# The expert layer as one block with its two norms: top four by the 8-largest instruction, token shares spread over partitions by transfers, the store in pieces

## What is computed

```python
x = _layernorm(x + _L1_attn_ref(x, ...))
# _L1_ffn_ref, x is (2048, 128):
scores = sigmoid(xt @ gate_w.T)                    # 16 experts
_, idx = lax.top_k(scores + gate_b, 4)             # of equal values the lower index wins
w = take_along_axis(scores, idx); w = w / sum(w) * 2.5
comb = zeros((T, 16)).at[arange(T)[:, None], idx].add(w)
for e in range(16):                                # w13 (128, 128), w2 (128, 64) each
    gate, up = split(xt @ w13[e].T, 2)             # 64 and 64 columns
    y = y + comb[:, e, None] * ((silu(gate) * up) @ w2[e].T)
y = y + _silu_and_mul(xt @ w13_s.T) @ w2_s.T       # the shared expert
x = _layernorm(x + y)
```

## Time and profile before

| | us |
|---|---|
| median of three runs | 2155.22 |
| the runs | 2154.92 to 2158.52 |
| the profiled execution's own time | 2151.45 |
| its span, first to last instruction | 2149.6 |
| attention's last addition ends, the second norm begins | 1961 |
| first product of block `eb` | 2015.5 |
| last output product ends | 2132.8 |

### The profile page before, as it was taken

The page is one execution under the profiler, slowest core; times in us unless marked ns, Lnnn a source line. Parts: engine busy times, 40 slices in busy tenths (PEclk is TensorE's granted clock), DMA queues, the critical chain, the costliest instruction groups (busy, mean ns, idle before and its releaser), DMA issues. The chain is left out here.

```text
span 2149.6 us, 36221 instructions
## 1 busy us (share of the span) xinstructions
PE 1897.5 (88%) x11462; PEld 938.7 (44%) x11462; DVE 1628.3 (76%) x2430; ACT 1257.6 (59%) x2587; POOL 1077.7 (50%) x1225
## 2 busy tenths in 40 slices
PE   5755898989846999999999999999999999993596
PEld 2543485558532444443444443444443444432254
DVE  6787765776555888887888887888887888872644
ACT  5523684568312777776777776777776777761111
POOL 0635642664106656666566565565664665661000
PEclk9988899989977999999999999999999999996698
DMA  1001210030025998988989998999998989991000
GB/s 36 1 1 66 50 30 30 6 74 6 13 90 212 342 336 328 330 328 320 329 327 334 332 336 293 335 333 336 329 326 308 333 325 343 335 328 60 0 1 20
DMA packets 197387, 444.03 MB, mean 207 GB/s; under 512 B 11904, under 2 KB 159232, under 8 KB 196160
## 3 DMA queue, kind: packets, MB, share of 16 engines
q1 hardware_dynamic: 197184, 441.54, 57.7%
HBM read 220.77 MB, written 206.70 MB: 199 GB/s over the span
## 5 line engine op out<-in xcount | busy, mean ns | idle before, releaser
L1602 ACT ACTIVATE g.probs<-g_score,g.lowest 128x1024 f32<-128x1024 f32 x514 | 568.4, 1110 | 331.1 <-DVE g.lowest L1588 331.1
L1588 DVE TENSOR_REDUCE g.lowest<-g_score 128x1 f32<-128x1024 f32 x514 | 605.5, 1219 | 187.5 <-PE g_score L1556 187.5
L1556 PE MATMUL g_score<-g.keys,g.queries 64*128 64x512 f32 x2056 | 501.8, 607 | 22.4 <-issue 11.6
L1688 DVE STREAM_TRANSPOSE g.blocks<-g.probs 128x768 f32<-128x768 f32 x512 | 467.1, 950 | 1.0
L1618 PE MATMUL g_mix_ps<-g.far,mid.y_tok 128*64 128x512 f32 x1584 | 382.8, 605 | 0.0
L1556 PEld LDWEIGHTS g_score<-g.keys,g.queries 64*128 64x128 f32 x2056 | 183.9, 187 | 253.2 <-ACT g.probs L1602 130.9
L1648 POOL TENSOR_TENSOR g.scaled<-g.scaled,g.coef 128x1024 f32<-128x1024 f32 x67 | 127.1, 1897 | 251.0 <-ACT g.scaled L1640 243.2
L1708 POOL TENSOR_TENSOR mid.y_tok<-mid.y_tok,g.waves 128x512 f32<-128x512 f32 x128 | 162.4, 1269 | 75.9 <-ACT mid.y_tok L1571 75.9
L1461 POOL TENSOR_TENSOR g.queries<-mid.y_tok 64x256 f32<-64x256 f32 x256 | 185.5, 725 | 19.7
L1578 PEld LDWEIGHTS g_turned<-top.ident,g.probs 128*128 128x128 f32 x1024 | 107.7, 141 | 195.5 <-issue 195.5
L1578 PE MATMUL g_turned<-top.ident,g.probs 128*128 128x128 f32 x1024 | 168.5, 287 | 0.0
(11 more groups left out here) (362 smaller groups left out, 2834.2 us busy)
## 6 DMA issues: line engine op xcount, KB each, us to landing
g.far<-bounce SPq DMA_DIRECT2D x257, 768.0 KB, 7.0
bounce<-g.blocks SPq DMA_DIRECT2D x256, 768.0 KB, 6.3
g.far<-g.near SPq DMA_DIRECT2D x7, 768.0 KB, 6.7
lt0.v_late<-la0.v SPq DMA_DIRECT2D x6, 512.0 KB, 10.1
lt1.v_late<-la1.v SPq DMA_DIRECT2D x6, 512.0 KB, 10.0
bounce<-g.near SPq DMA_DIRECT2D x4, 768.0 KB, 9.4
top.upto<-stored_mixers SPq DMA_DIRECT2D x33, 64.0 KB, 6.6
lt.turns<-turns SPq DMA_DIRECT2D x1, 2048.0 KB, 7.9
```

What stands on the lines that cost most here:

```text
L1556: nc.tensor.matmul(score[:, 2 * pair + odd], queries[rows, turn, head, cols], keys[rows, turn, head, pair * CH:(pair + 1) * CH], start=Tru ...
L1588: nc.vector.tensor_reduce(lowest[:, unit, half, r:r + 1], score[:, 2 * half:2 * half + 2].rearrange("p b n -> p (b n)"), AX.X, ALU.max, ne ...
L1602: nc.scalar.activation(probs[:, r % 2, half * 2 * CH:(half + 1) * 2 * CH], score[:, 2 * half:2 * half + 2].rearrange("p b n -> p (b n)"), ...
L1688: ins = nc.vector.transpose(blocks[:, r, :, REST * half:REST * (half + 1)].rearrange("p j t c -> p t j c"), probs[:, r % 2, at:at + REST * ...
```

## The change

The second norm, the experts, the last norm and the store become one block.

- DVE normalises tile by tile and signals each (`x_ready`); PE turns and routes chunk by chunk, in an order written out. Each ACT table is loaded ahead by a small activation (`warm`).
- The four best are found with `nc.vector.max`, which gives the eight largest of a token's 16 values, one instruction per tile. What is above the fourth value is taken; of what equals it, the first so many as are missing, by a running count over the 16 places. These steps stand between the multiplies of chunk 0.
- The shares are turned while chunk 1 runs, copied by ACT, stored to DRAM, and loaded again spread over 64 partitions each (`share`), four transfers of 1 MB for each half of the tokens. The weighing (`weigh`) moves to chunks 2 and 3, two groups per unit.
- The shared expert's up weights fill the unused half of its gate weights.
- The outputs stand behind the units of chunks 2 and 3, and four at the end. Twelve tiles are normalised and stored ahead of the last four.

```diff
-    normalise(nc, "n2", acc, x)
...
+                by_row = shares.rearrange("(g a) n -> a g n", a=2)
+                for half in range(2):
+                    at = slice(half * 2 * CH, (half + 1) * 2 * CH)
+                    sync.wait_ge(m["comb_copied"], half + 1)
+                    sync.dma_start(shares[:, at], combT[:, at]).then_inc(shares_stored[half], 16)
+                    sync.wait_ge(shares_stored[half], 16)
+                    for c in (2 * half, 2 * half + 1):
+                        cols = slice(c * CH, (c + 1) * CH)
+                        for a in range(2):
+                            sync.dma_start(share[64 * a:64 * a + 64, :, cols],
+                                           by_row[a:a + 1, :, cols].broadcast_to([64, SHARED, CH]))\
+                                .then_inc(share_loaded[c], 16)
+                to = out.rearrange("(t p) d -> p t d", p=P)
+                sync.wait_ge(m["normed"], 12)
+                sync.dma_start(to[:, 0:12], x[:, 0:12]).then_inc(stored, 16)
+                sync.wait_ge(m["normed"], T)
+                sync.dma_start(to[:, 12:T], x[:, 12:T]).then_inc(stored, 16)
...
+                def up(n):
+                    c, g = divmod(n, GROUPS)
+                    cols = slice(c * CH, (c + 1) * CH)
+                    if n >= 2:
+                        pe.wait_ge(m["mult_done"], n - 1)
+                    nc.tensor.matmul(g_ps[:, n % 2], w_gate[:, g], xT[:, cols], start=True, stop=True)\
+                        .then_inc(m["g_done"], 1)
+                    if g < SHARED:
+                        nc.tensor.matmul(u_ps[:, n % 2], w_up[:, g], xT[:, cols], start=True, stop=True)\
+                            .then_inc(m["u_done"], 1)
...
+                turn(0)
+                turn(1)
+                pe.wait_ge(m["loaded"], 2 * 16)
+                route(0)
+                turn(2)
+                route(1)
+                turn(3)
+                route(2)
+                route(3)
+                pe.wait_ge(m["w_loaded"], 3 * 16)
+                for c in range(NC):
+                    for g in range(GROUPS):
+                        up(c * GROUPS + g)
+                        if c == 1 and g == 0:
+                            pe.wait_ge(m["comb_ready"], 1)
+                            turn_comb(0)
+                        if c == 1 and g == 2:
+                            pe.wait_ge(m["comb_copied"], 1)
+                            turn_comb(1)
+                        if c == 2 and g >= 5:
+                            down(g - 5)
+                        if c == 3 and g < 4:
+                            down(4 + g)
+                        if c == 3 and g >= 5:
+                            down(8 + g - 5)
+                for t in range(12, T):
+                    down(t)
...
+                def weigh(c, g):
+                    cols = slice(c * CH, (c + 1) * CH)
+                    if g == 0:
+                        dve.wait_ge(share_loaded[c], 32)
+                    dve.wait_ge(m["mult_done"], c * GROUPS + g + 1)
+                    nc.vector.tensor_tensor(hidden[:, g, cols], hidden[:, g, cols], share[:, g, cols], ALU.mult)\
+                        .then_inc(m["weighed"], 1)
...
+                for c in range(NC):
+                    for g in range(GROUPS):
+                        multiply(c * GROUPS + g)
+                        if c == 0:
+                            if g == 0:
+                                count_equal()
+                            elif g == 1:
+                                run_count()
+                            elif g == 2:
+                                choose()
+                            elif g == 3:
+                                share_out()
+                        if c == 2:
+                            if g < 4:
+                                weigh(0, 2 * g)
+                                weigh(0, 2 * g + 1)
+                            elif g < 8:
+                                weigh(1, 2 * g - 8)
+                                weigh(1, 2 * g - 7)
+                            if g >= 6:
+                                add(g - 6)
+                        if c == 3:
+                            if g < 4:
+                                weigh(2, 2 * g)
+                                weigh(2, 2 * g + 1)
+                                add(3 + g)
+                            elif g < 8:
+                                weigh(3, 2 * g - 8)
+                                weigh(3, 2 * g - 7)
+                                if g == 4:
+                                    add(7)
+                            if g >= 6:
+                                add(8 + g - 6)
+                measure(0, 10)
+                add(11)
+                measure(10, 12).then_inc(m["var3_ready"], 1)
+                add(12)
+                dve.wait_ge(m["std3_ready"], 1)
+                nc.vector.reciprocal(spread3[:, 0:12], spread3[:, 0:12]).then_inc(m["inverse3_ready"], 1)
+                add(13)
+                dve.wait_ge(m["inverse3_ready"], 1)
+                for t in range(6):
+                    centre(t)
+                add(14)
+                for t in range(6, 12):
+                    centre(t)
+                add(15)
+                measure(12, T).then_inc(m["var3_ready"], 1)
...
+    a["w_gate"][:, GROUPS - 1, HID_E:] = a["w_up_e"][:, GROUPS - 1, 0:HID_E]
```

More of the change, by code:

```diff
@@ new lines, in experts @@
+        router = sp.sb("router", [P, E])
+        rows = sp.sb("rows", [P, E])
+        hidden = sp.sb("hidden", [P, GROUPS, S])
+        share = sp.sb("share", [P, SHARED, S])
+        gated = sp.sb("gated", [P, 2, CH])
+        combT = sp.sb("combT", [E, S])
+        score = sp.sb("score", [P, T, E])
+        biased = sp.sb("biased", [P, T, E])
+        best = sp.sb("best", [P, T, 8])
+        beyond = sp.sb("beyond", [P, T, TOP - 1])
+        quota = sp.sb("quota", [P, T])
+        equal = sp.sb("equal", [P, T, E])
@@ new lines, in experts @@
+        shares = nc.dram_tensor("shares", (E, S), F32).ap()
+        turned = sp.ps("turned", [P, 2, CH])
+        g_ps = sp.ps("g_ps", [P, 2, CH])
+        u_ps = sp.ps("u_ps", [P, 2, CH])
+        prod = sp.ps("prod", [P, 2, CH])
+        score_ps = prod[:, 1, 0:T * E]
+        m = {n: sp.sem(n) for n in ("w_loaded", "loaded", "eps_ready", "stats_done", "var_ready", "std_ready", "inverse_ready",
+                                    "x_ready", "turn_done", "xT_ready", "score_done", "score_ready", "zeroed", "order",
+                                    "comb_ready", "comb_turned", "comb_copied", "shares_stored0", "shares_stored1",
+                                    "share0", "share1", "share2", "share3", "g_done", "u_done", "silu_ready", "mult_done",
+                                    "weighed", "prod_done", "added", "stats3_done", "var3_ready", "std3_ready",
+                                    "inverse3_ready", "normed")}
@@ new lines, in _ @@
+                ins.then_inc(m["var_ready"], 1)
+                dve.wait_ge(m["std_ready"], 1)
+                nc.vector.reciprocal(spread[:], spread[:]).then_inc(m["inverse_ready"], 1)
+                dve.wait_ge(m["inverse_ready"], 1)
+                for t in range(T):
+                    nc.vector.tensor_scalar(x[:, t], acc[:, t], moments[:, t, 0:1], spread[:, t:t + 1],
+                                            ALU.subtract, ALU.mult).then_inc(m["x_ready"], 1)
+                dve.wait_ge(m["loaded"], 2 * 16)
@@ L2168, in build @@
             if stages >= 4:
-                experts(nc, dram, const, y_tok)
-            last = y_tok
-            with nc.Block() as block:
-                @block.sync
-                def _(sync):
-                    sync.dma_start(out.rearrange("(t p) d -> p t d", p=P), last[:]).then_inc(stored, 16)
-                    sync.wait_ge(stored, 16)
+                experts(nc, dram, const, x_tok, y_tok, out, stored)
 def _layout(i):
```

318 lines of the change are left out of this document (154 added, 164 removed).

## The result

The median went from 2156.42 us (four runs, 2154.92 to 2158.52) to **2093.39 us** (four runs, 2089.8 to 2096.33): ratio 0.9706, with a 95% interval of 0.9685 to 0.9728. The forecast was 2090.4, so 64.8 us were forecast and 63.0 came. The profiled execution took 2090.94 us with a span of 2089.1.

A forecast was written before the change was run, and what follows sets the result against it. DVE's choice of experts holds everything up for 30.4 us, then PE is full until the output products end. Gains 36.7 + 18.8 + 10.3 = 65.8 us, less 1 for hand-overs: 2155.2 - 64.8 = 2090.4 us, range 2084 to 2107.

The forecast's parts named there:

- The front: Second norm, routing and search until the first gate product: it starts at 1978.85 instead of 2015.54, gaining 36.7 us.
- The products: First gate product to last output product: 95.3 us of PE work plus 3.2 of stalls, 98.5; gains 18.8 us.
- outputs 16 x 2.01 = 32.2: PE's work in the products: sixteen tiles' output products at the kernel before's 2.01 us each, 32.2 us.
- All are in time: Share loads for chunks 0 to 3 land before DVE asks, chunk 1 by 0.7 us only; costed at 0.
- C: Time when the first half of the shares is copied, in chunk 1, about 2001.5; store and loads are timed from it.
- 2.1/0.225 = 9.3 us: Loading one chunk's 2.1 MB of shares at 225 GB/s, the rate of attention's move of v: 9.3 us.
- rival 1: Late shares: loads reading one row 64 times flow at 125 GB/s, 16.5 us a chunk; 2109 us, chance 0.14.
- The clock: Cold start of PE in the products: 6.0 us at half clock as before, costing 3.0 us.
- Stalls: PE waiting in the products: 1.4 us in chunk 0, 1.0 in chunk 2, 0.8 ahead of output 13.
- slower: Rival: share loads below 77 GB/s make the kernel slower than before; 2264 us at 38 GB/s, chance 0.03.
- PE's clock did not stay low through chunk 0: Rival claimed the opposite: PE's clock stays low through chunk 0, costing 12 us more; 2102 us, chance 0.06.
- the search was the bound: Rival claimed it was not: only the removed products and the end gain, 34 us; 2121 us, chance 0.02.

The follow-up runs named there:

- e1: Changed kernel with the ninth output product of each tile over all 128 rows instead of 64; median 2094.22 us, ratio 0.9709.
- e2: Changed kernel with all eight share loads issued at the block's start from a table, chunks 2 and 3 reading different rows; median 2094.71 us, ratio 0.9723.
- e7: Changed kernel with each load of shares writing every other partition instead of the lower or upper 64; median 2094.46 us, ratio 0.9726.
- e11: Changed kernel with shares loaded early from a table, as in e2, and written to every other partition; median 2090.15 us, ratio 0.9685.
- e9: Changed kernel with both halves of the shares turned in chunk 0 instead of chunk 1; median 2093.64 us, ratio 0.9697.
- e4: Kernel before, without the 32 products that spread the shares, weighing with xT instead; median 2137.02 us, ratio 0.9903.
- e3: Changed kernel with the whole choice of experts done before the first multiply instead of between multiplies; median 2102.41 us, ratio 0.9754.
- e5: Kernel before, with only the search replaced by the 8-largest instruction and running count, in its old place; median 2144.42 us, ratio 0.9939.
- e13: Changed kernel with shares turned early, ninth product over 128 rows, and the second share store issued by ACT instead of SP; median 2086.43 us, ratio 0.9672.

## Why the prediction held, step by step

**The front: right.** Forecast 17.54 us from attention's end, measured 16.84. The first gate product stood at 1979.17 (forecast 1978.85, with attention's end 1.0 us later than in the profile of before). What was taken as ready was ready, and a route, 3.43/2 = 1.71 us by the row at 1975.90, was taken as 1.75. The 8-largest instruction, which no row showed, runs 16 times in 1.32 us, 0.08 apart; I had 0.1. The estimate of 0.17 that the prediction worked out from VectorE: DVE Perf Modes in the Trainium skill (section on SBUF-source latency, a formula for tensor_tensor) did not serve better: by this trace it fits the 160 ns of one instruction and not the distance between two, which is what counts.

**The products: the mechanism right, the terms mis-sized.** Forecast 98.5, measured 104.14, 5.6 too long. The step that was furthest off is the first below.

- *The output products.* The step that failed is "outputs 16 x 2.01 = 32.2". In the kernel before, all nine products of a tile are over 128 rows, the ninth with an empty half; the change cuts the ninth to the 64 rows that hold something (`rows_g`), and I carried the 2.01 over. In after a tile costs 2.29 and its next gate product 0.11 more, and full rows restore both (e1): 6.1 us in all, more than the whole error. The sign stood in the trace of before, around the share product, which has 64 rows. PE's timeline there, a gate product, the share product, the up product and the next tile's output product:

```profile
2100.76 1.02 PE L2072 MATMUL eb_g_ps<-e.xT,e.w_gate 128*128 128x512 f32 x2
2101.72 0.50 PE L2075 MATMUL eb_c_ps<-e.parts,e.copy 64*128 64x512 f32 x1
2102.14 1.12 PE L2076 MATMUL eb_u_ps<-e.xT,e.w_up 128*128 128x512 f32 x2
2103.11 2.17 PE L2084 MATMUL eb_prod<-e.w_down,eb.hidden 128*128 128x128 f32 x18
```

  The share product itself takes 0.42 us, and the products ahead of it and behind it 0.96 and 0.97, where 0.86 is their time among their like the earlier trace rows: about 0.1 us on each side of a 64-row product. What makes it so no run shows. The forecast counts this as "switches" that go away with the share products and does not see that the change brings 16 new pairs of them.
- *Late shares.* "All are in time" was wrong for three of four chunks. The start was right (C at 2000.89 against 2001.5, the store landing in 1.9 against 2.3). The size that failed is the rate, "2.1/0.225 = 9.3 us": 174 GB/s over the first 4 MB, 161 first and 204 then. Chunk 0 was there at C + 17.3 (forecast 13.3), chunk 1 at C + 27.6 (22.6), chunk 2 at C + 43.2 (35). So rival 1 happened in part: its reason (one row read 64 times) is shown by e2, e7 and e11, its 125 GB/s was too low, and its price of 19 us far too high, since PE works on while DVE waits. It cost 2.0 us (e2, e9). The row chosen, shows another limit, the ports of 64 partitions, which e11 confirms for other data. By the prediction's own sign ("A DVE wait for a DMA there ... would prove it wrong") this part of it was wrong: there were three such waits.
- *The clock.* Forecast 6.0 us at half clock, measured 2.8, worth 1.6 us in the other direction. With the front equal to 0.02 us, the length at half clock was 2.8, 3.0, 3.3, 3.6, 3.8, 3.9, 4.0, twice 5.9 and 6.0 us in the changed kernel and its variants. It does not go with any edit, and with one profile each what sets it is not shown; it is a scatter of up to 1.6 us in a stretch. That it fell on the short side here is luck.
- *Stalls.* Chunk 0: 1.6 us for 1.4. Chunk 2: DVE's unit is 1.80 us (its multiplies start at 2029.71 and 2031.51), not 2.07, for the two weighings and the multiply do not depend on one another and overlap (two weighings take 1.29 us together). In e2, with the shares there, PE runs through chunk 2 without a stall, so the 1.0 forecast for it did not come, nor did the 0.8 ahead of output 13: PE's last five outputs follow one another.
- *Borders of chunks.* Where two gate products meet, behind chunks 0 and 1, they take 1.98 us together instead of 1.72, 0.5 us in all. The forecast did not have it.

98.5 + 6.1 + 2.0 - 1.6 + 0.2 - 1.8 + 0.5 = 103.9; 0.2 us of the 104.14 is not explained. The 20.2 us for the share products are 19.2 by e4.

**The tail: right.** Forecast 6.5, measured 5.79: the 256 KB store lands in 2.3 us, not 2.7, and the statistics of four tiles take 1.1, not 1.3. **The hand-overs**, one microsecond taken off for some forty of them, are inside the stretches already and are part of what is unexplained.

**The rest of the sum.** From attention's end to the span's end 123.5 us were forecast and 126.77 measured, 3.3 more. The median is 3.0 above the forecast. It came out closer than its largest part, partly by luck: the products' 5.6 us too much stand against 0.7 too much forecast for the front, 0.7 for the tail and 1.0 for the hand-overs, and the profiled run of after lay 2.5 us below its median where 3.8 was taken over from before.

Three readings in the prediction were slips that move nothing: in the earlier trace rows PE is busy 14.52 of 16 us, so its gaps are 9% and not a quarter; a chunk of 2.1 MB at 125 GB/s takes 16.8 us and not 16.5; and the two estimates for the 8-largest instruction are 1.2 us apart and not 1.1.

The other rivals: slower, by loads under 77 GB/s, did not come near; PE's clock did not stay low through chunk 0, but in e3 it fell in a pause of 3.23 us, so the thought behind that rival has substance (behind a pause of 2.14 us in e1 and of 1.13 in after it stayed at its higher level); and the search was the bound ahead, as e5's 11.4 us show.

## What to carry to other kernels

Move work off a bound engine's path by order first: of 37 us in the front, a faster instruction gave 11 and the place of the steps, with those left out, 26. When several edits share one pipeline, test them together as well as alone: full rows were worth 2.5 us (at the same clock) as long as the shares were late, and 4 once they were early. Take the rate of a transfer from a row with the same source pattern as well as the same destination, and look at what a small store is queued behind.

## What the runs showed that was not expected

- Reading one DRAM row for 64 partitions flows at 174 to 189 GB/s wherever it lands, with stretches at 159 to 161; different rows at 222 GB/s to one half of the partitions and at 391 to every other one (e2, e7, e11).
- A product over 64 rows behind eight over 128 adds 0.28 us to the tile and 0.11 to the gate product behind it, though it has half the rows; running it over 128 rows, half of them zero, takes both away (e1).
- The 8-largest instruction over 16 values starts every 0.08 us.
- Behind a pause of 3.23 us a gate product took 2.08 us for 1.02: the granted clock had gone back from 1.00 to 0.50 (e3).
- A 64 KB store behind 4 MB of loads in one queue holds the next loads for 21 us; from ACT's queue it lands in 10.2 (e13).
